# A new order of every engine's steps in a two-layer gated transformer kernel

## The reference, cut to what matters

```python
x = x + tanh(g_xattn[0]) * attention(ctx, ctx, layernorm(x))   # K and V from ctx, Q from layernorm(x)
x = x + tanh(g_ffn[0])   * moe(layernorm(x))                   # 8 experts, hidden 256, top 2, silu(w0) * w1, wo
x = x + tanh(g_xattn[1]) * cross_attention(layernorm(x), ctx)  # context-to-query and query-to-context, then W_l
x = x + tanh(g_ffn[1])   * bitlinear_ffn(x)                    # weights to -1, 0, 1, activations to 8 bits, inner 512
```

```python
score = einsum('bhij,bhkj->bhik', k, q) / sqrt(8)
attn = softmax(score, axis=1)                  # over h
out = einsum('bhik,bhij->bhjk', attn, v)
```

## Time and profile before

| | us |
|---|---|
| median of 3 runs | 398.3 |
| lowest and highest | 397.81, 398.43 |
| span of the profiled execution | 397.3 |

### The profile page before, as it was taken

The page is one execution under the profiler, slowest core; times in us unless marked ns, Lnnn a source line. Parts: engine busy times, 40 slices in busy tenths (PEclk is TensorE's granted clock), DMA queues, the critical chain, the costliest instruction groups (busy, mean ns, idle before and its releaser), DMA issues.

```text
span 397.3 us, 10407 instructions
## 1 busy us (share of the span) xinstructions
PE 324.9 (82%) x3326; PEld 284.0 (71%) x3326; DVE 313.1 (79%) x913; ACT 256.4 (65%) x726; POOL 299.1 (75%) x459
## 2 busy tenths in 40 slices
...
GB/s 161 289 192 210 81 36 21 116 17 16 88 115 34 29 41 128 19 56 63 108 15 47 68 87 29 61 6 131 33 16 1 28 15 2 2 29 14 2 13 13
DMA packets 34454, 24.17 MB, mean 61 GB/s; under 512 B 3617, under 2 KB 32097, under 8 KB 34401
## 3 DMA queue, kind: packets, MB, share of 16 engines
...
## 4 chain that ended last, share of the span: by engine, by line
PE 37%; POOL 25%; DVE 13%; issue 10%; ACT 7%; DMA 4%; SPq 3%; POOLq 0%; DVEq 0%; ACTq 0%
POOL tree L939 9%; PE ps_d L1448 8%; POOL attn L945 8%; PE ps_z L1188 4%; PE ps_a L1196 3%; PE ps_z L1189 3%; PE ps_z L1190 3%; POOL m_h L876 2%; DVE head_max L1584 2%; DMA wf_raw<-in_wd 2%; DVE m_u L1623 1%; DMA k_rows<-rows_dram 1%; DVE y L1655 1%; PE ps_sc L1234 1%; DVE shifted L1590 1%
## 5 line engine op out<-in xcount | busy, mean ns | idle before, releaser
L1188 PE MATMUL ps_z<-m_xhi,w_hi 128*128 128x256 f32 x240 | 76.9, 320 | 12.7 <-DVE m_h L1631 6.1
L945 POOL TENSOR_TENSOR attn<-attn,head_inv 128x1024 f32<-128x1024 f32 x32 | 75.8, 2371 | 0.2 <-DVE head_inv L1606 0.2
L1448 PE MATMUL ps_d<-wdn,m_h 128*128 128x128 f32 x512 | 71.4, 283 | 4.7 <-DVE m_h L1631 2.1
L1448 PEld LDWEIGHTS ps_d<-wdn,m_h 128*128 128x128 f32 x512 | 63.1, 194 | 8.5 <-issue 4.1
L1189 PE MATMUL ps_z<-m_xhi,w_lo 128*128 128x256 f32 x240 | 68.8, 287 | 0.0
L1190 PE MATMUL ps_z<-m_xlo,w_hi 128*128 128x256 f32 x240 | 68.6, 286 | 0.0
L1623 DVE SCALAR_TENSOR_TENSOR m_u<-m_tanh,ps_z 128x256 f32<-128x256 f32 x120 | 49.0, 411 | 17.6 <-ACT m_tanh L1033 16.7
L1033 ACT ACTIVATE m_tanh<-ps_z 128x256 f32<-128x256 f32 x120 | 45.9, 384 | 26.0 <-PE ps_z L1190 25.6
L1188 PEld LDWEIGHTS ps_z<-m_xhi,w_hi 128*128 128x128 f32 x240 | 46.7, 195 | 19.3 <-issue 6.1
L876 POOL TENSOR_TENSOR m_h<-m_u,m_z 128x256 f32<-128x256 f32 x56 | 41.1, 734 | 17.2 <-DVE m_u L1623 17.2
L939 POOL TENSOR_TENSOR tree<-tree 128x256 f32<-128x256 f32 (+2 forms) x90 | 46.4, 515 | 7.1
...
## 6 DMA issues: line engine op xcount, KB each, us to landing
...
```

Of the source, the lines that this page charges most:

```text
L945: pool.tensor_tensor(e, e, head_inv[:, u % 2].unsqueeze(1).to_broadcast([P, HEADS, HALF]), ALU.mult).then_inc(s_attn, 1)
L1188: pe.matmul(dst, hi_w, hi_x, start=start, stop=False)
L1448: last = pe.matmul(ps_d[:, b * P:(b + 1) * P], m_h[:, m % 4, b * P:(b + 1) * P], wdn[:, m], start=(k == 0), stop=(k == TPE - 1))
```

## The change

Only the numbers in WHEN and ONCE are others, for all steps of all engines. The instructions, their waits, buffers and the number of spare matmuls are the same. Cut to the steps that are spoken of below:

```diff
-    "sp.load_a": (12, 1501, 2546, 3638, 7464, 12475, 17304, 20931),
+    "sp.load_a": (1, 653, 1579, 3362, 6301, 13136, 15630, 20671),
...
     "sp.store_parts": (
-        (1372, 2340, 5666, 9673, 12892, 17404, 21683, 25406),
-        (1416, 2436, 5877, 9884, 13964, 18240, 21883, 25695),
-        (1461, 3048, 6712, 10374, 14327, 18518, 22342, 26965),
-        (1671, 3218, 6753, 10415, 14367, 18559, 22433, 27006),
-        (1816, 3497, 6989, 10630, 14730, 18610, 22609, 27330),
-        (1891, 3739, 7086, 10786, 14806, 18653, 23156, 27406),
+        (834, 2049, 4584, 9124, 13230, 15583, 19496, 23526),
+        (931, 2096, 5279, 9171, 13277, 16313, 20222, 24313),
+        (1009, 2273, 5749, 9381, 13324, 16507, 20624, 24429),
+        (1056, 2609, 5796, 9077, 12306, 16266, 20269, 23588),
+        (1137, 2747, 5843, 9428, 12737, 16554, 20316, 24266),
+        (1215, 2888, 5890, 9522, 13089, 16648, 20577, 24476),
     ),
...
     "sp.fetch_rows": (
-        (1960, 3826, 7126, 11165, 15185, 19034, 23535, 27447),
-        (2176, 3979, 7280, 10827, 14847, 18694, 23197, 27600),
-    ),
+        (1262, 3004, 5937, 9886, 13503, 16695, 20765, 24570),
+        (1449, 3136, 6113, 9569, 13371, 16871, 20988, 24793),
+    ),
...
     "pool.head_sum": (
-        (3117, 4949, 8301, 12302, 16280, 20570, 24852, 28729),
-        (0, 5624, 9105, 13076, 17232, 21319, 25518, 29679),
-        (3829, 6030, 9761, 13649, 17656, 21891, 26017, 30177),
-        (0, 7157, 10779, 14947, 18951, 23148, 26958, 31135),
+        (2298, 4041, 7155, 11005, 14786, 18305, 22204, 25875),
+        (0, 4803, 8012, 11719, 15619, 19209, 22990, 26868),
+        (3050, 5094, 8421, 12576, 16639, 19995, 23991, 27606),
+        (0, 6326, 9513, 13221, 17072, 20853, 24562, 28041),
     ),
...
     "pool.head_norm": (
-        (3598, 5392, 8874, 12844, 17001, 21087, 25287, 29447),
-        (4134, 6411, 9529, 13951, 18081, 22533, 26394, 30483),
-        (4365, 7689, 11569, 15473, 19553, 23751, 27482, 31599),
-        (4596, 7995, 11800, 15901, 19859, 24178, 28349, 32128),
-    ),
+        (2816, 4569, 7588, 11486, 15195, 18976, 22756, 26515),
+        (3341, 5810, 8784, 12271, 15981, 19690, 23542, 27301),
+        (3574, 6617, 10087, 13796, 17577, 21358, 25147, 28688),
+        (3808, 6922, 10510, 14410, 18000, 21591, 25570, 28992),
+    ),
...
-    "pool.m_rstd": (5262, 8752, 12700, 16879, 20965, 25165, 29325, 33207),
+    "pool.m_rstd": (4451, 7822, 11367, 15076, 18857, 22638, 26239, 29877),
...
     "pool.m_h": (
-        (6337, 10074, 14182, 18004, 22194, 26320, 30714, 33831),
-        (6861, 10441, 14516, 18511, 22765, 26821, 31061, 34325),
-        (7078, 10515, 14799, 18778, 22945, 27399, 31522, 34691),
-        (7615, 11224, 15399, 19254, 23676, 27936, 31979, 35147),
-        (7921, 11495, 15704, 19785, 23982, 28011, 32359, 35331),
-        (8226, 12032, 16132, 20212, 24410, 28580, 32629, 35739),
-        (8678, 12605, 16683, 20891, 24612, 29067, 32791, 35999),
-    ),
+        (5385, 8712, 12200, 16358, 19924, 23920, 27230, 30500),
+        (5456, 9232, 12505, 16499, 20568, 24420, 27534, 30711),
+        (6043, 9373, 13149, 16930, 20711, 24491, 28403, 31154),
+        (6184, 9945, 13654, 17435, 21286, 25076, 28545, 31693),
+        (6850, 10320, 14030, 17929, 21943, 25499, 28921, 31846),
+        (7446, 10863, 14338, 18234, 22014, 25804, 29345, 32202),
+        (7517, 10934, 14714, 18596, 22495, 26166, 29475, 32465),
+    ),
...
-    "pool.y_res": (10367, 13574, 18312, 21817, 25821, 29981, 33448, 36784),
+    "pool.y_res": (9161, 12129, 15429, 20639, 23471, 27159, 30326, 33208),
...
-    "pool.g_rstd": (12106, 15779, 20090, 24057, 28227, 32433, 35617, 38044),
+    "pool.g_rstd": (10392, 14101, 17810, 21825, 25380, 29226, 32084, 34287),
...
-    "act.g_r": (12638, 16344, 20555, 24811, 29193, 32801, 36009, 38257),
+    "act.g_r": (10877, 14700, 18346, 22334, 26121, 29506, 32462, 34626),
...
     "act.o_raw": (
-        (15421, 19618, 23741, 27770, 31781, 34999, 37921, 0),
-        (16106, 20438, 24455, 28582, 32491, 35879, 38069, 0),
+        (14975, 18059, 21577, 25617, 29144, 32072, 34382, 0),
+        (15219, 18839, 22029, 26279, 29760, 32351, 34542, 0),
     ),
...
     "pe.kq": (
-        (477, 1835, 5419, 9492, 12622, 17139, 21304, 25292),
-        (1523, 3078, 6020, 10201, 14020, 17967, 21982, 26622),
+        (638, 1092, 4475, 7969, 11469, 15473, 19281, 22702),
+        (834, 2501, 4986, 8762, 12198, 16054, 19893, 23421),
     ),
...
     "pe.scores": (
-        (2658, 4507, 7807, 11692, 15800, 19673, 24064, 28170),
-        (3006, 4892, 8182, 12105, 16314, 20423, 24622, 28700),
-        (3359, 5356, 8859, 12590, 16978, 21092, 25459, 29224),
-        (3726, 5687, 9727, 13544, 17851, 21870, 26510, 30427),
-    ),
+        (1818, 3507, 6640, 10282, 13975, 17251, 21534, 25276),
+        (2189, 3886, 6959, 10707, 14513, 18102, 21897, 25670),
+        (2614, 4199, 7617, 11385, 15107, 18611, 22480, 26692),
+        (2942, 4944, 8169, 12044, 15926, 19551, 23457, 27081),
+    ),
...
-    "pe.v": (1319, 5085, 8891, 12379, 16864, 20787, 25115, 28897),
+    "pe.v": (1419, 4293, 7793, 11179, 15054, 18893, 22521, 26358),
...
-    "pe.f_at": (10437, 14429, 18637, 22942, 26854, 31083, 34431, 37359),
+    "pe.f_at": (9060, 12888, 16574, 20478, 24236, 27768, 31133, 33649),
...
-    "pe.f_c2q": (10839, 14988, 19118, 23275, 27450, 31440, 34833, 37574),
+    "pe.f_c2q": (9531, 13297, 17056, 20828, 24598, 28130, 31451, 33841),
...
     "pe.f_z": (
-        (11234, 15326, 19457, 23614, 27702, 31672, 35092, 37700),
-        (11293, 15401, 19532, 23745, 27931, 32016, 35224, 37805),
-    ),
+        (9787, 13553, 17295, 21095, 24928, 28313, 31731, 33964),
+        (9981, 13600, 17433, 21233, 24975, 28461, 31800, 34061),
+    ),
...
     "pe.g_pt": (
-        (14957, 18959, 23242, 27231, 31521, 34600, 37287, 38692),
-        (15840, 19811, 24184, 28210, 31986, 35543, 37968, 39255),
+        (14018, 17577, 20918, 25319, 28360, 31541, 34235, 35129),
+        (15029, 18449, 21674, 25786, 29203, 32175, 34427, 35403),
     ),
...
     "pe.g_down": (
-        (15379, 19509, 23666, 27531, 31650, 34728, 37523, 39412),
-        (16057, 20284, 24472, 28401, 32445, 35831, 38084, 39461),
-    ),
+        (14833, 17841, 21578, 25492, 29089, 31778, 34343, 35584),
+        (15148, 18705, 21783, 26232, 29723, 32291, 34557, 35640),
+    ),
...
-    "dve.a_stats": (251, 1983, 3025, 4213, 9586, 15340, 18880, 23501),
+    "dve.a_stats": (264, 1079, 2001, 4187, 9578, 13555, 16880, 20970),
...
     "dve.part_rest": (
-        (917, 2289, 5673, 9651, 13097, 17513, 21678, 25437),
-        (1721, 3345, 6709, 10371, 14216, 18179, 22507, 27113),
+        (834, 1680, 4596, 8252, 11620, 15604, 19557, 22822),
+        (1040, 2648, 5498, 9069, 12577, 16286, 20020, 23690),
     ),
...
     "dve.head_max": (
-        (2754, 4580, 7911, 11814, 15855, 19737, 24136, 28269),
-        (3106, 4841, 8253, 12227, 16373, 20596, 24693, 28772),
-        (3468, 5376, 9004, 12978, 17027, 21193, 25541, 29720),
-        (3897, 5899, 9805, 13673, 18289, 21918, 26660, 30809),
+        (1888, 3634, 6707, 10403, 14037, 17417, 21600, 25383),
+        (2343, 3874, 6947, 10862, 14639, 18277, 21954, 25755),
+        (2689, 4250, 7866, 11505, 15224, 18965, 22963, 26797),
+        (3101, 5383, 8438, 12213, 16327, 19825, 23990, 27509),
     ),
...
     "dve.head_shift": (
-        (2879, 4716, 8031, 11972, 16071, 20207, 24333, 28523),
-        (3232, 5205, 8456, 12346, 16615, 20808, 24871, 29039),
-        (3587, 5547, 9187, 13371, 17393, 21558, 25762, 29942),
-        (4094, 6254, 10205, 14394, 18499, 22612, 26779, 30981),
+        (2064, 3749, 6822, 10518, 14241, 17950, 21769, 25498),
+        (2489, 4061, 7252, 10977, 14754, 18446, 22244, 25994),
+        (2804, 4638, 8042, 11916, 15645, 19221, 23174, 26953),
+        (3216, 5831, 8954, 12783, 16452, 20225, 24149, 27783),
     ),
...
-    "sp.w_moe": 358,
-    "sp.w_out": 113,
-    "sp.w_fin": 1005,
-    "sp.w_ffn": 853,
-    "sp.w_late": 2804,
-    "pe.w_total": 1735,
-    "dve.w_lo": (2176, 5752),
-    "dve.w_abs": 1556,
-    "pe.warm_f": (36502, 36557, 36781, 37120, 37455, 37478, 37500, 37910, 37999, 38021, 38113, 38136, 38181, 38226),
-    "pe.warm_g": (38044, 38158, 38203, 38497, 38615, 38669, 39171, 39213, 39370, 39515, 39557, 39599, 39641, 39683),
-    "pe.warm_s": (2393, 2393, 2393, 2393, 2393, 2657, 2657, 3005, 3005, 3005, 3005, 3005, 3358, 3358, 3358, 3725, 3725, 3725, 3725, 3725, 3725, 3725, 3797, 3797, 3797, 3797, 3797, 3797, 3797, 3797, 3797, 3797, 3797, 3797, 3797, 4733, 5686, 5686, 6463, 6463, 6463, 6463, 7269, 7702, 9114, 9251, 9251, 9251),
+    "sp.w_moe": 470,
+    "sp.w_out": 235,
+    "sp.w_fin": 1673,
+    "sp.w_ffn": 94,
+    "sp.w_late": 3268,
+    "pe.w_total": 1335,
+    "dve.w_lo": (4483, 4788),
+    "dve.w_abs": 874,
+    "pe.warm_f": (32626, 32931, 33200, 33520, 33542, 33563, 33585, 33717, 33739, 33940, 34579, 34822, 34844, 34889),
```

(34 more changed lines are left out.)

166 lines of the change are left out of this document (80 added, 86 removed), and 202 rows, old and new, of the table WHEN.

## The result

The changed kernel takes 409.53 us (median of 4 runs, 405.70 to 412.41) where the kernel before, run beside it, takes 398.06 (397.55 to 398.43): a ratio of 1.0247 [1.0189, 1.0306], so slower. The ratio leaves out the run of 412.41, which fell in a slower state that executions of every kernel here can fall in. 370.9 was forecast. The profiled execution has a span of 407.4 us, 10.1 more than the one before.

What follows compares the result with a forecast made beforehand. POOL was the engine to follow in the long stage, with idle time to fill. Fill 5.5, long stage 18.9, last experts 0 and drain 3.0 sum to 27.4 us off the 397.3 span, plus 1.0 carried: 370.9 us, range 361 to 381.

Steps and rivals of the forecast that it cites:

- Fill: Before the first sum of attention rows: reordered loads and an earlier Q fetch save 5.5 us, range 2.5 to 8.5.
- I get the Q fetch about 6.1 us earlier, at 15.4: Fill, on SP: fewer issues ahead of the first store, and Q stores following at once, bring the Q fetch to 15.4.
- scores no earlier than 25: Sign in the fill that the forecast is wrong: the first scores come no earlier than 25 us.
- The long stage: First sum to the last pair's first up-projection: ready POOL steps fill POOL's waits, saving 18.9 us, range 6 to 25.
- the charge of 1.0 us for DVE beside POOL: Long stage: cost added for moving the first dve.w_lo beside a full POOL, where either engine can hold the other.
- So 25.4 - 5.5 = 19.9 us can go: Long stage: of POOL's 25.4 us waiting for others, all but 5.5 at three places with nothing to put in can go.
- My bound below, a third kept, or 6: Long stage's lower bound: waits come back in other places and only a third of the gain stays, 6 us.
- DMAs moved, costed at nothing: Stores and fetches on SP move with their steps; late fetches cost nothing, up to 2 us a pair in the range.
- Last experts: The last pair's expert stage, bound by PE, keeps its instructions: 0, with 1.5 us either way.
- Drain: Last 34.6 us: pe.f_c2q behind fewer steps (0.7) and a higher clock (up to 4.8) save 3.0 us; loss of 1 possible.
- another engine becomes the bound: Rival, chance 0.17: DVE and PE, nearly full in the long stage, cap the gain at 10.7 us, giving 387.6.
- the clock at 405: Rival, chance 0.03: spare matmuls run out earlier, the lower clock level halves PE from the first sum on, giving 405 us.

Runs made afterwards that it cites:

- E2: The changed kernel with pair 1's x and ctx loaded ahead of the expert weights: 403.48 us, ratio 1.0132 to the kernel before.
- E3: The changed kernel with both E1's nine-wide dve.weights and E2's early load of pair 1: 398.22 us, ratio 0.9965 to the kernel before.
- E10: E3 with sp.w_late earlier and pe.scores 0 of pair 1 behind the steps that followed it: 396.49 us, ratio 0.996 to the kernel before.
- E6: E3 with the expert weights loaded behind pair 0's fetches and the steps reading them moved back: 397.99 us, ratio 0.9987 to the kernel before.
- E1: The changed kernel with dve.weights' four small products writing nine values instead of eight: 401.3 us, ratio 1.0041 to the kernel before.
- E4: The kernel before with E1's nine-wide dve.weights, as control: 399.04 us, ratio 0.9998.
- E9: E7 with sp.w_late earlier and pe.scores 0 of pair 1 behind the steps that followed it: 398.52 us, ratio 0.9997 to the kernel before.
- E7: E6 with 56 spare matmul steps in all, laid where PE waits in the start: 397.89 us, ratio 0.999 to the kernel before.

## Why the prediction was wrong

*Fill, forecast -5.5, measured +4.3.* The step that failed is "I get the Q fetch about 6.1 us earlier, at 15.4". I counted SP's own issues and let the Q stores "follow at once". Their data were late: I had not gone along ACT's list, where a step of pair 1 waiting for a load behind 2 MB of weights stood ahead of pair 0's part 2. E2, E3 and E10 show that (3.2 to 4.8 us at the first sum). E6 shows that 14.40 was to be had, without the bulk load. My "wrong" sign, scores no earlier than 25, came up. My kept distance from fetch to scores, 6.1 us, was about right where nothing else stood between (6.3 in E2); in the changed kernel pe.v made it 9.6.

*The long stage, forecast -18.9, measured +6.6.* Two steps failed. The first is the charge of 1.0 us for DVE beside POOL. I applied the rule to the one instruction whose move I had in view, and that one was held for 0.6 us; but small DVE instructions with their data in SBUF were held as well, beside the fuller POOL. The excess is 16.5 us (19.1 less 2.6), most of it in dve.weights and in the rounding, and E1, with E4 as its control, shows 8.2 us of run time from dve.weights alone. The second is "So 25.4 - 5.5 = 19.9 us can go". Free of the late load and of most of that harm (an excess of 7.5 us is left, in other small instructions), E10's POOL has 1.9 us less idle time, not 19.9. The waits I listed ended in DVE and ACT results. In E10 the one for m_mv is as long as before (3.9), and others came, for f_mv, g_mv and head_inv (2.6, 4.0 and 1.8, before 0.0, 0.8 and 0.2). My bound below, a third kept, or 6, was too high as well. I had chosen POOL by its busy time and let its idle time stand for time of the run. The page's chain of the work that ended last, which I did not use, gave POOL a quarter of the span before the change, and less after it:

```profile
PE 37%; POOL 25%; DVE 13%; issue 10%; ACT 7%; DMA 4%; SPq 3%; POOLq 0%; DVEq 0%; ACTq 0%
```
```profile
PE 44%; DVE 22%; issue 11%; POOL 7%; ACT 7%; DMA 5%; SPq 4%; DVEq 0%; ACTq 0%; POOLq 0%
```

That a loop between the engines sets the pace, in which a POOL step put in front of one wait delays the step behind it and DVE then waits for that, is argued from these rows; no run shows it by itself.

*Where in the stage the 6.6 us are.* From pair 0's first sum to pair 2's 53.3 us passed before and 59.4 after, with POOL busy for 48.2 and 48.1: +6.2. From there to pair 7's, 201.5 and 203.5: +2.0. The rest, to the last pair's up-projection, 48.2 and 46.6: -1.6. The start keeps most of its loss without the two harms (59.3 in E3). E10's two edits went with 57.0, but the same two took nothing off in E9 (59.9, E7 59.2), so the cause of this loss stays open.

*DMAs moved, costed at nothing.* PE's waits at the scores for q_rows were 5.7 us in the stage, where the kernel before had 0.5, for k_rows: inside the 2 us a pair that I left in the range, and outside the sum.

*Last experts, forecast 0, measured +1.1,* inside the 1.5 I allowed. PE is busy for 28.3 of the 29.05 us, at a granted clock of 0.94 where it was 1.00; that the clock made the difference is not shown.

*Drain, forecast -3.0, measured -1.9.* The mechanism was right, and the clock's term was mis-sized. From pe.f_c2q to pe.f_z of the last pair the same 24 matmuls (the rows count one or two others) ran at either level of the clock, first before the change, then after it:

```profile
373.83:379.10 5.27, 5.27 (x26) 5.24 (x25) 0.74 (x4) 2.91 (x8) 0.91 (x2) 0.50 0.01 3
```
```profile
385.72:389.12 3.40, 3.37 (x25) 2.89 (x25) 2.16 (x9) 2.92 (x10) 0.87 (x2) 1.00 0.02 5
```

The 5.27 us at 1.2 GHz became 3.40 at 2.4 GHz. That is the whole gain: behind it 18.2 us passed before and 18.3 after, and ahead of it, from the last y to f_c2q, 11.1 and 11.0. So the clock gave 1.9, where I had credited it with 2.3 and thought 4.8 possible, and the 0.7 for f_c2q's place behind fewer steps came to 0.1.

*The rivals.* The nearest is "another engine becomes the bound": DVE grew to 275.4 of the stage's 309.6 us, but I let it cap the gain and gave it no price of its own, so its sign was wrong. The rival on the slow side, the clock at 405, had a time near the measured one and the wrong mechanism, so its nearness is luck: the clock was lower in the stretch it named (0.69 for 0.87 from 20 to 58 us), but E3 undoes the slowdown with 0.54 there. That 95% lay on "faster" came from terms that were all gains of order, with one charge of 1.0 us for what filling POOL does to its neighbour.
